# The causal triangle of the first attention's row maxima: from TensorE mask matmuls to fused VectorE instructions

## The chip, the cores and the metric

One core of a Trainium2 chip runs the whole program. The metric is the device time of one execution in microseconds (us); a lower one is better. The core has TensorE (PE, with its weight loads as PEld), VectorE (DVE), ScalarE (ACT), GpSimd (POOL) and a queue of DMA issues on SyncE (SP). Each works through its own instructions in order, and they wait for each other by semaphores.

## The reference

The program is a two-layer block. Only the attention of the first layer is touched:

```
xn = layernorm(x)                         # x: 8 sequences of 256 rows, 256 columns
q, k, v = split(xn @ W_qkv)               # 16 heads of 16
attn = q @ k.T / 4 + alibi_bias + causal_mask   # -inf where j > i
attn = softmax(attn)
s = (attn @ v) @ W_o
x = x + s * silu(ffn0(xn))
# then the second layer: attention of 16 heads of 128, a mixture of experts, x = x + s * silu(...)
```

## The kernel before

The first layer runs as eight batches, one for each sequence, from about 20 to 400 us of the span; `batch(b, ...)` of each engine writes the order out by hand. A batch holds the projections, the attention, the feed-forward (`up`, `down`, with `hidden` on VectorE), the normalisation of the finished sequence b - 1 and its router. The 16 heads form 4 groups of 4; the heads of a group lie on 32 partitions each, so the four matmuls of a group use four quarters of the array.

Softmax needs each query's maximum over its allowed keys. The kernel computes the scores twice. First, `scores(b, g)` on TensorE puts queries on partitions: for each head bank `six[:, h]` takes 256 columns for the late queries (128 to 255, all keys) and 128 columns for the early ones (0 to 127, the first 128 keys). In each of the two the last 128 columns are the diagonal block, where the triangle applies. `maxima(b, g)` on VectorE takes the negated maxima into `nmax`; `maxima_T` on TensorE transposes them (line 433); `queries_max` on VectorE adds them to the queries as a further row (line 1276, `qB`); and `scores_T` on TensorE computes the scores again, with keys on partitions, the maximum already subtracted and its own mask matmuls (line 440), for ScalarE's exponential. The chain within a group is thus TensorE, VectorE, TensorE, VectorE, TensorE, and the orders by hand put other work between the links.

On TensorE, between scores and maxima_T stand: in group 0 two projections of 12 matmuls each; in group 1 the mix of group 0, one `up` of 12 matmuls and two transposes; in group 2 the same kind; in group 3 also the router's six logit matmuls. On VectorE, the maxima stand in group 0 behind the last router step, in group 1 behind `gate_s` (line 1316), in group 2 behind the normalisation of the former sequence (`normalise`, line 1241, which waits for rs of GpSimd), and in group 3 behind the normalisation of the next sequence. In groups 0 and 1 VectorE has little queued ahead of the maxima, in groups 2 and 3 it has a good deal.

The semaphores: `s0_ps` says that a group's scores are there, `max0` that its maxima are, `nmaxT_ps` that they are transposed, and `exp0` that ScalarE has read the transposed scores, before which `scores` must not write the banks again. `three` (lines 390 to 392) is a product in three matmuls, of high and low parts.

Of the kernel before, what the change touches and what calls it, by code (L numbers as in the profile page):

```python
# [25 lines left out]
BF16 = mybir.dt.bfloat16  # L26
ALU = mybir.AluOpType
ACT = mybir.ActivationFunctionType
AX = mybir.AxisListType

P = 128
NB, T, D = 8, 256, 256
TT, KD = T // P, D // P
NT = NB * TT
H0, E0 = 16, 16
GH = 4
NG = H0 // GH
VW = P // GH
# [17 lines left out]
def build(nc, x, pack_qk, pack_vo, pack_w1, pack_w3, pack_w2, pack_attn, pack_experts, pack_shared, gate_b, q_norm, k_norm,  # L56
          rope_cosT, rope_sinT, ident_c, hadamard_c, tri_add_c, tri_mul_c, q_row_c, k_rows_c, before_c, route_c, out):
    ctx = ExitStack()
    with ctx:
        def sem(name):  # L60
            return ctx.enter_context(nc.semaphore(name))
# [5 lines left out]
        six = ctx.enter_context(nc.psum_tensor("six", [P, 6, 512], F32))  # L67
# [16 lines left out]
        def region(start, end):  # L84

            at = [start]

            def put(name, shape, dt=F32):
                size = math.prod(shape[1:]) * (2 if dt == BF16 else 4)
                t = nc.alloc_sbuf_tensor_at(name, shape, dt, offset=at[0])  # L90
                at[0] += (size + 31) // 32 * 32
                assert at[0] <= end, (name, at[0], end)
                return t
            return put
# [4 lines left out]
        sa = region(LOW, LATE)  # L99
# [3 lines left out]
        w2_h, w2_l = sa("w2_h", [P, NJ, D], F32R), sa("w2_l", [P, NJ, D], F32R)  # L103
        w2_a = sa("w2_a", [P, NJ * D])
        hadamard_r = sa("hadamard_r", [P, P], F32R)
        ident_b, tri_add, tri_addT = sa("ident_b", [P, P], BF16), sa("tri_add", [P, 2, P], BF16), sa("tri_addT", [P, 2, P], BF16)
        q_row, k_rows = sa("q_row", [P, 1]), sa("k_rows", [P, NG, T])
        cosT_sb, sinT_sb, norm_w = sa("cosT_sb", [P, H1]), sa("sinT_sb", [P, H1]), sa("norm_w", [P, 2])
        st0, mv0, ve0, rs0 = sa("st0", [P, TT, 6]), sa("mv0", [P, TT, 2]), sa("ve0", [P, TT]), sa("rs0", [P, TT])
# [2 lines left out]
        qA, qB, kA = sa("qA", [P, NG, T]), sa("qB", [P, NG, T]), sa("kA", [P, NG, T])  # L112
        nmax = sa("nmax", [P, TT, P])
# [9 lines left out]
        sa = region(LATE, TOP)  # L123
# [88 lines left out]
        xT0l_sb, xT1l_sb, max0, z0_sb, hid_sb, hidl_sb = (sem(n) for n in (  # L212
            "xT0l_sb", "xT1l_sb", "max0", "z0_sb", "hid_sb", "hidl_sb"))
# [26 lines left out]
        def after(eng, s, value):  # L240

            if isinstance(value, int) and value <= 0:
                return
            eng.wait_ge(s, value)
# [12 lines left out]
        hadamard, tri_add32 = y0[:, 0, 0:P], y0[:, 0, P:2 * P]  # L257
# [129 lines left out]
        def _(pe):  # L387
# [25 lines left out]
            def scores(b, g):  # L413

                pe.wait_ge(qA_sb, 2 * b + g // 2 + 1)
                pe.wait_ge(kA_sb, 2 * b + g // 2 + 1)
                after(pe, exp0, 4 * b + g)
                for h in range(GH):
                    pe.matmul(six[:, h, P:3 * P], ident_b[:], tri_add[:].rearrange("p c k -> p (c k)"),
                              start=True, stop=False, skip_group_check=True)  # L420
                for h in range(GH):
                    r = slice(h * VW, (h + 1) * VW)
                    pe.matmul(six[:, h, 0:T], qA[r, g, P:T], kA[r, g, :], start=False, stop=True, skip_group_check=True)
                for h in range(GH):
                    r = slice(h * VW, (h + 1) * VW)
                    last = pe.matmul(six[:, h, T:T + P], qA[r, g, 0:P], kA[r, g, 0:P], start=False, stop=True,
                                     skip_group_check=True)
                last.then_inc(s0_ps, 1)

# [135 lines left out]
            def batch(b, par, first, final):  # L565
                t = b - 1
                if first:
                    pe.wait_ge(consts_made, 1)
                scores(b, 0)
                pe.wait_ge(kA_sb, 2 * b + 1)  # L570
                queries(b, 1)
# [12 lines left out]
                if not first:  # L584
                    project_out(t, banks[0][:, :])
                scores(b, 1)
                mix(b, 0, par)
                if first:
# [21 lines left out]
                after(pe, gf_sb, b)  # L610
                down(b, 0)
                scores(b, 2)
                mix(b, 1, par)
                pe.wait_ge(hid_sb, 8 * b + 2)
# [57 lines left out]
            t = NB - 1  # L672
# [529 lines left out]
        def _(dve):  # L1202
# [61 lines left out]
            def maxima(b, g):  # L1264

                dve.wait_ge(s0_ps, 4 * b + g + 1)
                after(dve, nmaxT_ps, 4 * b + g)
                dve.tensor_reduce(out=nmax[:, 1, E0 + 1::VW], in_=six[:, 0:GH, 0:T], axis=AX.X, op=ALU.max, negate=True)
                dve.tensor_reduce(out=nmax[:, 0, E0 + 1::VW], in_=six[:, 0:GH, T:T + P], axis=AX.X, op=ALU.max,
                                  negate=True).then_inc(max0, 1)  # L1270

            def queries_max(b, g):

# [124 lines left out]
            def batch(b, first, final):  # L1398
# [6 lines left out]
                def ffn_lo(n, wl, wh):  # L1405
                    dve.wait_ge(wa_hi, n + 1)
                    lo(wl[:].rearrange("p k c -> p (k c)"), raw[:, n % 2, :], wh[:].rearrange("p k c -> p (k c)"))\
                        .then_inc(wa_lo, 1)

                maxima(b, 0)  # L1410
                if not first:
                    gate_out(t)
# [5 lines left out]
                if first:  # L1418
                    ffn_lo(2, w1_l, w1_h)
                    ffn_lo(3, w3_l, w3_h)  # L1420
                maxima(b, 1)
                beside(0)
                queries_max(b, 1)
# [12 lines left out]
                if not first:  # L1436
                    normalise(t, xn1, mv1, rs1, rs1_sb, xn1_sb)
                maxima(b, 2)
                queries_max(b, 2)
                hidden(b, 3)  # L1440
# [27 lines left out]
            norm_T0(0)  # L1468
            dve.wait_ge(consts_loaded, 16 * N_CONST)
            dve.tensor_copy(ident_b[:], ident[:])  # L1470
            dve.tensor_copy(tri_add[:], tri_add32[:].unsqueeze(1).to_broadcast([P, 2, P]))
            dve.tensor_scalar(out=tri_addT[:], in0=tri_mul[:].unsqueeze(1).to_broadcast([P, 2, P]), scalar1=1.0,
                              scalar2=1e30, op0=ALU.subtract, op1=ALU.mult)
            dve.tensor_copy(hadamard_r[:], hadamard[:])
# [16 lines left out]
            t = NB - 1  # L1491
# [446 lines left out]
```

## Time and profile before

| | |
|---|---|
| time, median of 3 runs | 1307.63 us (1307.0 to 1309.41) |
| the profiled execution | 1307.02 us, span 1305.2 us |
| mean granted TensorE clock | 0.985 |
| TensorE busy | 1234.5 us, 95% of the span |
| VectorE busy | 865.4 us, 66% |
| ScalarE busy | 599.8 us, 46% |
| GpSimd busy | 490.9 us, 38% |
| chain that ended last | PE 86%, DVE 8%, ACT 2%, issue 2% |

The page gives the busy time of each engine, with matmul ends modelled; the chain that ended last is followed back from the last instruction, at each step to what released it. A timeline lists instructions in order of start, with the idle time of the engine before them and what ended it in square brackets. A row marked x4 or x8 holds several instructions: its duration runs from the first start to the last end, so that it overlaps the row that follows.

### The profile page before, as it was taken

The numbers are of one execution on the slowest core, as the hardware profiler recorded it, in microseconds if no ns is written. First come the engines' busy times: TensorE is split into PE (matmuls) and PEld (weight loads), VectorE is DVE, ScalarE is ACT, GpSimd is POOL, SyncE is SP. The second block draws the span as 40 slices with busy tenths as digits, with TensorE's granted clock in tenths as the row PEclk, the third lists the DMA queues.
The fourth block names the chain that finished last, engine by engine and source line by source line (L and its number), as shares of the span: only waits on it lengthen the run. The fifth ranks groups of instructions, "written<-read, shape, count | busy, mean of one in ns | idle before, by whom it ended". The sixth has DMA issues, their size and how long they took to land.

```text
span 1305.2 us, 25390 instructions
## 1 busy us (share of the span) xinstructions
PE 1234.5 (95%) x9326; PEld 1083.8 (83%) x9326; DVE 865.4 (66%) x1733; ACT 599.8 (46%) x1351; POOL 490.9 (38%) x488
## 2 busy tenths in 40 slices
PE   5699999999998789999989999999999999999996
PEld 4588888888887667777768999999999999999995
DVE  4647667667666744434457878888887766777685
ACT  3333333333433345555545555454554545555452
POOL 0122432442341400000027766767675444454441
PEclk9799999999999989999999999999999999999998
DMA  6764144234102943333330111102010000000010
GB/s 212 266 230 154 66 154 154 91 128 162 42 34 98 353 159 105 103 105 105 103 114 28 62 30 56 34 25 65 26 58 9 32 2 1 2 1 1 1 33 33
DMA packets 63672, 112.18 MB, mean 86 GB/s; under 512 B 6976, under 2 KB 36032, under 8 KB 62016
## 3 DMA queue, kind: packets, MB, share of 16 engines
q1 hardware_dynamic: 57408, 93.79, 20.5%
q0 software_dynamic: 6144, 16.79, 4.0%
q8 instruction: 77, 1.26, 0.4%
q14 instruction: 43, 0.35, 0.1%
HBM read 49.86 MB, written 60.69 MB: 85 GB/s over the span
## 4 chain that ended last, share of the span: by engine, by line
PE 86%; DVE 8%; ACT 2%; issue 2%; DMA 0%; POOL 0%; SPq 0%; POOLq 0%; DVEq 0%; ACTq 0%
PE bank L703 7%; PE six L720 6%; PE bank L781 4%; PE bank L779 4%; PE bank L780 4%; PE six L817 4%; PE bank L390 4%; PE bank L392 3%; PE bank L391 3%; PE bank L852 2%; PE bank L854 2%; PE bank L853 2%; PE bank L792 2%; PE bank L791 2%; PE bank L793 2%; PE six L818 2%
## 5 line engine op out<-in xcount | busy, mean ns | idle before, releaser
L1604 DVE TENSOR_TENSOR sq<-xs 128x512 f32<-128x512 f32 x128 | 131.1, 1025 | 39.2 <-ACT xs L1147 39.2
L1801 POOL TENSOR_TENSOR rstd<-msq,half_pow 128x8 f32<-128x8 f32 x64 | 105.9, 1655 | 96.2 <-DVE msq L1611 94.3
L1128 ACT ACTIVATE pT<-six,rstd 128x256 f32<-128x256 f32 x128 | 60.7, 475 | 172.1 <-PE six L818 172.1
L1813 POOL TENSOR_TENSOR pT<-pT,tri_mul 128x512 f32<-128x512 f32 x64 | 82.0, 1281 | 147.2 <-ACT pT L1175 147.2
L1738 POOL TENSOR_TENSOR hid_l<-hid,hid_h 128x256 fp32r<-128x256 f32 x64 | 48.0, 750 | 229.4 <-ACT hid_h L950 229.4
L703 PE MATMUL bank<-experts,xT 128*128 x316 | 109.8, 470 | 0.8 <-ACT xT L1072 0.8
L779 PE MATMUL bank<-bw_h,xT1h 128*128 128x512 f32 x256 | 105.6, 412 | 0.7 <-issue 0.7
L781 PE MATMUL bank<-bw_l,xT1h 128*128 128x512 f32 x256 | 100.3, 392 | 0.0
L780 PE MATMUL bank<-bw_h,xT1l 128*128 128x512 f32 x256 | 100.0, 390 | 0.0
L1213 DVE TENSOR_TENSOR yT1l<-six,yT1h 128x512 fp32r<-128x512 f32 x64 | 44.2, 691 | 83.0 <-ACT yT1h L1180 83.0
L1804 POOL TENSOR_TENSOR qn<-xs,rstd 128x256 f32<-128x256 f32 x128 | 91.5, 736 | 5.0
L1606 DVE TENSOR_REDUCE ssq<-sq 128x4 f32<-128x512 f32 x128 | 87.8, 686 | 4.4
L1152 ACT ACTIVATE v<-bank 128x512 f32<-128x512 f32 x64 | 38.3, 598 | 109.1 <-PE bank L793 109.1
L1147 ACT ACTIVATE xs<-bank 128x512 f32<-128x512 f32 x128 | 78.1, 610 | 11.7 <-PE bank L781 4.3
L720 PE MATMUL six<-experts,zT 128*128 x316 | 81.5, 380 | 1.2 <-DVE zT L1553 1.2
L852 PE MATMUL bank<-bw_h,yT1h 128*128 128x256 f32 x256 | 77.9, 304 | 3.8 <-DVE yT1l L1213 3.8
L1833 POOL DMA_INDIRECT yg<-cells_scratch,slots_all x64 | 75.5, 1180 | 14.8 <-issue 14.8
L1839 POOL MEMSET v<- 128x16 f32 x1 | 0.1, 125 | 214.5 <-PE six L720 214.5
L390 PE MATMUL bank<-xT0h,w_h 128*128 128x256 f32 x256 | 76.0, 297 | 2.7 <-DVE w_l L1213 2.5
L817 PE MATMUL six<-qT,kT 128*128 128x256 f32 x256 | 76.4, 380 | 2.1 <-ACT qT L1169 1.2
L1553 DVE COPY zT<-six 128x256 f32<-128x256 f32 x95 | 40.3, 424 | 56.7 <-PE six L711 56.7
L791 PE MATMUL bank<-bw_h,xT1h 128*128 128x256 f32 x256 | 77.3, 302 | 0.0
(282 smaller groups left out, 3934.6 us busy)
## 6 DMA issues: line engine op xcount, KB each, us to landing
cells_scratch<-zeros SPq DMA_DIRECT2D x8, 4352.0 KB, 14.8
xg<-cells_scratch SPq DMA_DIRECT2D x79, 128.0 KB, 2.0
cells_scratch<-y SPq DMA_DIRECT2D x79, 128.0 KB, 1.7
experts<-pack_experts_dram SPq DMA_DIRECT2D x16, 608.0 KB, 11.8
raw<-pack_attn_dram SPq DMA_DIRECT2D x8, 1024.0 KB, 5.3
raw<-pack_w_dram SPq DMA_DIRECT2D x2, 1024.0 KB, 4.9
xT_scratch<-xT1h_c SPq DMA_DIRECT2D x8, 256.0 KB, 2.1
xT_scratch<-xT1l_c SPq DMA_DIRECT2D x8, 256.0 KB, 2.9
```

The costliest lines, as they stand in the source:

```text
L390: pe.matmul(o, wh, mh, start=first, stop=False)
L703: last = pe.matmul(banks[j % 2][:, 0:2 * HE], xT[:, j % 2, k, :], weights(e, k * 2 * HE, 2 * HE), start=k == 0, stop=k == KD - 1)
L720: last = pe.matmul(six[:, 4 + r, 0:D], zT[:, r, c, :], w, start=c == 0, stop=c == 1)
L779: pe.matmul(banks[tt][:, :], xT1h[:, k, c], w[0][:, k, :], start=k == 0, stop=False)
L780: pe.matmul(banks[tt][:, :], xT1l[:, k, c], w[0][:, k, :], start=False, stop=False)
L781: last = pe.matmul(banks[tt][:, :], xT1h[:, k, c], w[1][:, k, :], start=False, stop=k == KD - 1)
L791: pe.matmul(o[:, tt, :], xT1h[:, k, c], w[0][:, k, :], start=k == 0, stop=False)
L817: pe.matmul(s_b[:, 0, h * T:(h + 1) * T], kT1[:, r, h, 0:P], qT1[:, r, h, :], start=True, stop=True)
L852: pe.matmul(o[:, tt, :], yT1h[:, r, h, c], w[0][:, h, :], start=h == 0, stop=False)
L1604: dve.tensor_tensor(out=sq[:, tt, :], in0=x_qk, in1=x_qk, op=ALU.mult).then_inc(sq_sb, 1)
L1801: pool.tensor_tensor(out=rstd[:, r, :], in0=msq[:, r, :], in1=half_pow[:], op=ALU.pow).then_inc(rstd_sb, 1)
L1804: last = pool.tensor_tensor(out=qn[:, r, tt, :, :], in0=xs[:, r, tt, 0, :, :], in1=rstd[:, r, 4 * tt:4 * tt + 2].unsqueeze(2).to_broadcast ...
```

## The change

`scores` no longer begins with four mask matmuls (identity times triangle, bf16, 256 columns, one per head); the score matmuls start their banks themselves. `maxima` no longer takes two reductions over the four heads together, of 1024 and 512 elements per partition. It issues, for each head and each half, one fused instruction: it adds the mask (now float, 256 wide, its first half zero), multiplies by -1, writes the result back over the scores in PSUM, and keeps the minimum, which is the negated maximum, in an accumulator that goes to one column of `nmax`. `scores_T` keeps its own mask matmuls.

```diff
@@ buffers
-        ident_b, tri_add, tri_addT = sa("ident_b", [P, P], BF16), sa("tri_add", [P, 2, P], BF16), sa("tri_addT", [P, 2, P], BF16)
+        ident_b, tri_add, tri_addT = sa("ident_b", [P, P], BF16), sa("tri_add", [P, T]), sa("tri_addT", [P, 2, P], BF16)
@@ TensorE, scores
                 for h in range(GH):
-                    pe.matmul(six[:, h, P:3 * P], ident_b[:], tri_add[:].rearrange("p c k -> p (c k)"),
-                              start=True, stop=False, skip_group_check=True)
+                    r = slice(h * VW, (h + 1) * VW)
+                    pe.matmul(six[:, h, 0:T], qA[r, g, P:T], kA[r, g, :], start=True, stop=True, skip_group_check=True)
                 for h in range(GH):
                     r = slice(h * VW, (h + 1) * VW)
-                    pe.matmul(six[:, h, 0:T], qA[r, g, P:T], kA[r, g, :], start=False, stop=True, skip_group_check=True)
-                for h in range(GH):
-                    r = slice(h * VW, (h + 1) * VW)
-                    last = pe.matmul(six[:, h, T:T + P], qA[r, g, 0:P], kA[r, g, 0:P], start=False, stop=True,
+                    last = pe.matmul(six[:, h, T:T + P], qA[r, g, 0:P], kA[r, g, 0:P], start=True, stop=True,
                                      skip_group_check=True)
                 last.then_inc(s0_ps, 1)
@@ VectorE, maxima
-                dve.tensor_reduce(out=nmax[:, 1, E0 + 1::VW], in_=six[:, 0:GH, 0:T], axis=AX.X, op=ALU.max, negate=True)
-                dve.tensor_reduce(out=nmax[:, 0, E0 + 1::VW], in_=six[:, 0:GH, T:T + P], axis=AX.X, op=ALU.max,
-                                  negate=True).then_inc(max0, 1)
+                for h in range(GH):
+                    e = h * VW + E0 + 1
+                    for t, s, mask in ((1, six[:, h, 0:T], tri_add[:]), (0, six[:, h, T:T + P], tri_add[:, P:T])):
+                        last = dve.tensor_tensor_reduce(out=s, in0=s, in1=mask, scale=-1.0, scalar=1e30, op0=ALU.add,
+                                                        op1=ALU.min, accum_out=nmax[:, t, e:e + 1])
+                last.then_inc(max0, 1)
@@ VectorE, constants
-            dve.tensor_copy(tri_add[:], tri_add32[:].unsqueeze(1).to_broadcast([P, 2, P]))
+            dve.memset(tri_add[:, 0:P], 0.0)
+            dve.tensor_copy(tri_add[:, P:T], tri_add32[:])
```

TensorE, from the last `down` matmul ahead of group 2's scores to the mix of group 1 (`pT`, `v`), before:

```order
L478 MATMUL six<-w_l,hid_h 128x256
L419 MATMUL six<-tri_add,ident_b 128x256 [waits exp0,kA_sb,qA_sb]
L419 MATMUL six<-tri_add,ident_b 128x256 x3
L423 MATMUL six<-kA,qA 128x256 x4
L426 MATMUL six<-kA,qA 128x128 x4
L458 MATMUL six<-pT_80,v_78 32x256 [waits y0_sb,exp0]
```

The same place in the changed kernel, where code behind the edit has a line number smaller by three:

```order
L475 MATMUL six<-w_l,hid_h 128x256
L420 MATMUL six<-kA,qA 128x256 [waits exp0,kA_sb,qA_sb]
L420 MATMUL six<-kA,qA 128x256 x3
L423 MATMUL six<-kA,qA 128x128 x4
L455 MATMUL six<-pT_80,v_78 32x256 [waits y0_sb,exp0]
```

The four mask matmuls are gone, their waits stand at the first score matmul, and nothing else has moved.

VectorE, from the normalisation ahead of group 2's maxima to the addition to the queries, before:

```order
L1241 TENSOR_SCALAR xn_97<-x_all,mv_93,rs_95 128x256 [waits rs1_sb]
L1241 TENSOR_SCALAR xn_97<-x_all,mv_93,rs_95 128x256
L1268 TENSOR_REDUCE nmax<-six 128x4 [waits nmaxT_ps,s0_ps]
L1269 TENSOR_REDUCE nmax<-six 128x4
L1276 TENSOR_TENSOR qB<-six,qA 128x256 [waits sT0_ps,nmaxT_ps]
```

And now, the first head of four (the rows from `six,nmax` to the second `nmax` stand four times in all, the later three without a wait); a row that only writes `nmax 128x1` is the read of the accumulator, an instruction of its own:

```order
L1238 TENSOR_SCALAR xn_97<-x_all,mv_93,rs_95 128x256 [waits rs1_sb]
L1238 TENSOR_SCALAR xn_97<-x_all,mv_93,rs_95 128x256
L1268 ISA six,nmax<-six,tri_add 128x256 [waits nmaxT_ps,s0_ps]
L1268 ISA nmax 128x1
L1268 ISA six,nmax<-six,tri_add 128x128
L1268 ISA nmax 128x1
```

Two instructions have become sixteen at the same place in the queue, between the same neighbours.

## Rows read from the trace of the kernel before

**Rows 1.** Page, busy us (share of the span) and instructions of each engine:

```profile
PE 1234.5 (95%) x9326; PEld 1083.8 (83%) x9326; DVE 865.4 (66%) x1733; ACT 599.8 (46%) x1351; POOL 490.9 (38%) x488
```

**Rows 2.** Windows view: stretch, length, busy us by engine, clock, DMA share:

```profile
core 0: us, PE busy (x) PEld busy (x) DVE busy (x) ACT busy (x) POOL busy (x), PEclk, DMA share, GB/s
60.00:400.00 340.00, 330.81 (x3437) 288.53 (x3436) 222.63 (x556) 127.23 (x265) 109.81 (x134) 1.00 0.34 124
```

**Rows 3.** Waits of TensorE, 92 to 400 us: total, times, longest:

```profile
PE bank L400 <- DVE hid L1287: 4.5, 6, 0.8
PE bank L390 <- DVE xT0l L1213: 3.1, 6, 0.5
```

**Rows 4.** Timeline of TensorE, 140 to 183 us: start, duration, instruction:

```profile
140.46 0.28 PE L533 MATMUL bank<-wvo_l,yT0h 128*128 128x256 f32 x1
140.58 0.61 PE L419 MATMUL six<-tri_add,ident_b 128*128 128x256 bf16 x4
141.12 0.71 PE L423 MATMUL six<-kA,qA 32*128 32x256 f32 x8
141.66 0.40 PE L426 MATMUL six<-kA,qA 32*128 32x128 f32 x8
...
144.53 0.38 PE L433 MATMUL six<-ident,nmax 128*128 128x128 f32 x2
...
150.92 0.40 PE L426 MATMUL six<-kA,qA 32*128 32x128 f32 x8
...
153.79 0.38 PE L433 MATMUL six<-ident,nmax 128*128 128x128 f32 x2
...
167.34 0.28 PE L392 MATMUL bank<-xT0l,w_h 128*128 128x256 f32 x1
167.56 0.64 PE L458 MATMUL six<-pT,v 128*32 128x256 f32 x8
...
182.85 0.38 PE L433 MATMUL six<-ident,nmax 128*128 128x128 f32 x2
```

**Rows 5.** Timeline of VectorE, 142 to 182 us, idle before in brackets:

```profile
142.12 1.23 DVE L1268 TENSOR_REDUCE nmax<-six 128x4 f32<-128x1024 f32 x1 [0.59 <-PE six L426]
143.26 0.68 DVE L1269 TENSOR_REDUCE nmax<-six 128x4 f32<-128x512 f32 x1
144.95 0.43 DVE L1276 TENSOR_TENSOR qB<-six,qA 128x256 f32<-128x256 f32 x1 [1.01 <-PE six L433]
...
145.74 0.42 DVE L1287 TENSOR_TENSOR hid<-bank,th 128x256 f32<-128x256 f32 x1
146.08 0.20 DVE L1293 RECIPROCAL rden<-six 128x8 f32<-128x8 f32 x1
...
147.60 0.14 DVE L1223 COPY waited<-ident 128x1 f32<-128x1 f32 x1
147.66 0.74 DVE L1225 BATCH_NORM_STATS2 st<-x_all 128x6 f32<-128x256 f32 x2
148.44 0.15 DVE L1228 COPY waited<-st 128x1 f32<-128x1 f32 x1
148.51 0.24 DVE L1230 BATCH_NORM_AGGREGATE mv<-st 128x2 f32<-128x6 f32 x2
...
151.07 0.73 DVE L1241 TENSOR_SCALAR xn<-x_all,mv,rs 128x256 f32<-128x256 f32 x2 [0.34 <-POOL rs L1723]
151.72 1.22 DVE L1268 TENSOR_REDUCE nmax<-six 128x4 f32<-128x1024 f32 x1
152.86 0.68 DVE L1269 TENSOR_REDUCE nmax<-six 128x4 f32<-128x512 f32 x1
...
155.57 0.29 DVE L1296 TENSOR_TENSOR y<-six,rden 128x128 f32<-128x128 f32 x1
155.78 0.74 DVE L1225 BATCH_NORM_STATS2 st<-x_all 128x6 f32<-128x256 f32 x2
...
181.15 0.68 DVE L1269 TENSOR_REDUCE nmax<-six 128x4 f32<-128x512 f32 x1
```

## The prediction

> **What bounds the kernel now.** I read the page's busy shares first: TensorE is busy for 1234.5 us, 95% of the span of 1305.2 us [rows 1]. The changed code runs only in the first attention, whose 32 groups (8 batches, 4 groups of 4 heads) lie between 20 and 400 us. From 60 to 400 us, TensorE is busy 330.8 of 340 us at a granted clock of 1.00 (2.4 GHz) and VectorE 222.6 us, 65% [rows 2]. So the question is not whether VectorE has room on average, for it has, but whether it has room between the two points where TensorE needs its answer. The waits of TensorE from 92 to 400 us say where it stands today: 4.5 us for hid and 3.1 us for xT0l, both at the end of a batch, and nothing for the maxima [rows 3]. Third, I read the two engines' timelines through one batch, the third (b = 2), from 132 to 180 us, and into group 0 of the next, and measured for each group how long after VectorE's last maximum TensorE comes to transpose it. That slack decides the case.
>
> **What is removed on TensorE.** Per group, four mask matmuls. In row order the last projection starts at 140.46, the first mask matmul at 140.58 and the first score matmul at 141.12, so the four hold the queue for 0.54 us [rows 4]. Something of that returns: a 4-byte matmul of 32 rows or columns behind the three-pass projections starts 0.22 us after the last of them (167.34 to 167.56) where the mask matmul started after 0.12 us, so 0.10 us comes back [rows 4]. The gain, G, is 0.54 - 0.10 = 0.44 us per group, 14 us over 32 groups, if all of it were on the path.
>
> **What is added on VectorE.** Two instructions per group become sixteen: four fused ones of 256 elements, four of 128 and, behind each, a one-column read of the accumulator; the order of the changed kernel shows them. No row of the trace shows the fused instruction or that read, so both are bounded by neighbours.
>
> The old pair takes from 142.12 to 143.26 + 0.68 = 143.94, that is 1.82 us [rows 5]. For the new chain the spacing of starts counts, since neighbours without a wait overlap: a 256-element two-input instruction lasts 0.42 us, but the next starts 0.34 us after it (145.74, 146.08); one of 128 elements lasts 0.29 us and the next starts after 0.21 us (155.57, 155.78); a one-column instruction lasts 0.14 to 0.15 us and the next starts after 0.06 to 0.07 us (147.60, 147.66; 148.44, 148.51) [rows 5]. I take 0.34, 0.21 and 0.07: 4 x (0.34 + 0.21) + 7 x 0.07, and 0.14 for the last read in full, is 2.83 us. The maxima then come E = 2.83 - 1.82 = 1.01 us later after their start.
>
> The bounds of E: if every fused instruction and every read must end before the next starts, 4 x (0.42 + 0.29) + 8 x 0.14 = 3.96 us and E = 2.14. If the reads cost nothing, 4 x 0.55 + 0.08 = 2.28 us and E = 0.46. As the far end below, if only elements cost anything: the two reductions start 1.14 us apart for 1024 elements, 1.1 ns each, so 1536 elements take 1.7 us and E = -0.1. I stay near the spacing rows, since they are of the same engine, the same sizes and likewise without waits.
>
> The Trainium skill (Vector Engine (DVE) Microarchitecture Reference, Measured stream behaviour on trn2) gives 1.0417 ns per column and about 75 ns per instruction after overlap. As an estimate that makes 1536 x 1.0417 ns + 16 x 75 ns = 2.80 us of starts, about 2.88 us to the end of the last read, E = 1.06; the time would then be 1319.5 us instead of the forecast below. No row here shows the read itself.
>
> **What of it lies on the path.** The maxima end; TensorE transposes them (L433); VectorE adds them to the queries (L1276); TensorE computes the transposed scores. Allowing 0.05 us from one engine to the other (the transposes end at 144.53 + 0.38, the addition starts at 144.95), the slack ahead of L433 is [rows 4, 5]:
> - group 0: maxima end 181.15 + 0.68 = 181.83, L433 at 182.85: 0.97 us
> - group 1: 143.94, L433 at 144.53: 0.54 us
> - group 2: 152.86 + 0.68 = 153.54, L433 at 153.79: 0.20 us
> - group 3 stands as group 2 does: 0.20 us
>
> Here is the choice that matters: which groups keep G. In groups 0 and 1, VectorE idles until the scores arrive (0.59 us before group 1's maxima, released by L426 [rows 5]), so the maxima start earlier when the mask goes. Group 0 keeps 0.40 us of G, group 1 all 0.44 us. In group 2 the scores are there at 150.92 + 0.40 = 151.32, but the maxima start at 151.72, behind the normalisation (L1241), which waited for GpSimd's rs and before that for the last group's transposes [rows 4, 5]. That chain does not move with the mask. TensorE comes 0.44 us earlier to a transpose whose input is later by E: the gain turns into waiting. Group 3's maxima stand behind the other normalisation in the same way.
>
> A batch therefore moves by -0.40 - 0.44 + (E - 0.97) + (E - 0.54) + 2 x (E - 0.20), a bracket below zero counting as zero in the first two. With E = 1.01: -0.84 + 0.04 + 0.47 + 1.62 = +1.29 us. Nothing absorbs it behind: the end of the batch is a chain ScalarE, VectorE (router), TensorE, which starts from group 3's scores, and its two waits [rows 3] move along whole. Eight batches taken alike are +10.3 us. The first batch differs (the weights' butterfly is on VectorE, its maxima of group 1 are fully on the path) and the last has no second normalisation; I set these off against each other.
>
> **Edits at nothing.** The float mask is made by a memset and a copy in place of one cast, in the start-up. The matmuls' start flags change no duration. The scores written back to PSUM have no reader, since the transposed scores overwrite them after max0. The DMAs are as they were, and code after 400 us is the same; it moves as a whole.
>
> The profiled execution took 1307.02 us (span 1305.2 us and 1.8 us around it), 0.6 us under the median of 1307.63 us. On the median the forecast is 1307.6 + 10.3 = 1317.9, **1318 us**.
>
> **The rivals.** By the same line for a batch, times eight:
> - **The reads are exposed.** Each main instruction drains before its read, E = 2.14: -0.84 + 1.17 + 1.60 + 3.88 = 5.81 us per batch, 46 us, 1354 us. For it: the accumulator is complete only with the last element. Against it: all rows of neighbours without a wait overlap by 0.08 us [rows 5]. The Trainium skill (VectorE: DVE Perf Modes, The DRAIN you can't avoid) says that the next operation does not start until the pipe is empty; by that rule this rival holds, and the trace speaks against it, with starts 0.34 us apart where one lasts 0.42 us. Chance 0.15, spread from 1337 to 1354 us.
> - **Writing scores back in place in PSUM halves the rate.** Then 1536 x 1.1 ns = 1.7 us more, E = 2.7 and about 8 us per batch, some 1371 us. No VectorE row writes PSUM, so nothing speaks for it. Chance 0.03.
> - **Cheap reads: nothing much changes.** E = 0.46 gives -0.84 + 0.52 = -0.32 us per batch, 1305 us; E = 0.7 gives +0.32 us, 1310 us. It needs reads under about 0.03 us; no one-column row is that short. Chance 0.13.
> - **Faster: TensorE's gain survives.** The point is E = 0.59, where 3E = 0.84 + 0.54 + 0.40: if the new chain takes under 2.41 us from first start to last end, TensorE's 0.44 us in groups 0 and 1 outweigh the waits in groups 2 and 3. With E = -0.1 the maxima are never late in groups 0 and 1, and groups 2 and 3 give 0.3 us each: -1.44 us per batch, 1296 us. For it: 95% busy TensorE [rows 1] and 14 us less work there. Against it: 1536 elements and eight fixed costs already make 2.28 us before any read. Chance 0.07.
>
> **How the numbers follow.** The forecast (E from 0.7 to 1.6, 1310 to 1337 us) has 0.62. About 0.2%, 2.6 us, is what a measurement of this kernel can tell from no change: that is 1305.0 to 1310.2 us. Faster has 0.08 (the last rival and the edge of the one before), the same 0.12, slower 0.80. The range of 1306 to 1345 us leaves out some 0.08 below and 0.12 above.
>
> **What the changed profile would show.** TensorE busy falls by the mask matmuls, about 14 us by its queue; new waits of TensorE at the transposes of the maxima, none in group 0, about 0.5 us in group 1 and E - 0.20 + 0.44 = 1.25 us in groups 2 and 3, 3 us per batch and 24 us in all; VectorE's group from first start to last end 2.8 us; each batch after the first 1.3 us longer; nothing changed after the attention. Wrong would be: starts of the fused instructions spaced by more than 0.36 us or the reads by more than 0.09 us (then dearer), or a VectorE start in groups 2 and 3 that follows the scores and not the normalisation (then G is kept there too).

## The result and the profile after

The changed kernel takes 1313.55 us (median of 5 runs, 1313.16 to 1315.22), the one before 1307.63 us: 5.9 us or 0.46% slower, ratio 1.0046 with a 95% interval of 1.0031 to 1.0061. The forecast was slower by 10.3 us. The span of the profiled execution went from 1305.2 to 1312.1 us.

The page after, busy time of each engine as in [rows 1], and the chain that ended last by engine:

```profile
PE 1229.0 (94%) x9198; PEld 1078.9 (82%) x9198; DVE 891.4 (68%) x2182; ACT 600.0 (46%) x1351; POOL 489.7 (37%) x488
PE 76%; DVE 15%; ACT 4%; issue 3%; POOL 1%; DMA 0%; SPq 0%; ACTq 0%; DVEq 0%; POOLq 0%
```

128 matmuls are gone, VectorE has 449 rows more, and the chain has moved: TensorE carried 86% of it before, now 76%, and VectorE 15% in place of 8%. The maxima themselves (L1268) are 4% of it.

The forms of the new work, line, engine, operation, count, busy us and mean ns of one:

```profile
L1268 DVE CUSTOM_DVE_ANT_0 six<-six,tri_add 128x256 f32<-128x256 f32 x128 | 58.5, 457 | 5.4 <-PE six L423 4.5
L1268 DVE CUSTOM_DVE_ANT_0 six<-six,tri_add 128x128 f32<-128x128 f32 x128 | 42.5, 332 | 0.0
L1268 DVE DVE_READ_ACCUMULATOR2_ANT nmax<- 128x1 f32 x256 | 36.4, 142 | 0.0
```

What counts is the distance of starts. VectorE's timeline in group 1 of the third batch, which answers to the first rows of [rows 5]:

```profile
143.14 0.43 DVE L1268 CUSTOM_DVE_ANT_0 six<-six,tri_add 128x256 f32<-128x256 f32 x1
143.49 0.14 DVE L1268 DVE_READ_ACCUMULATOR2_ANT nmax<- 128x1 f32 x1
143.49 0.33 DVE L1268 CUSTOM_DVE_ANT_0 six<-six,tri_add 128x128 f32<-128x128 f32 x1
143.74 0.14 DVE L1268 DVE_READ_ACCUMULATOR2_ANT nmax<- 128x1 f32 x1
143.74 0.47 DVE L1268 CUSTOM_DVE_ANT_0 six<-six,tri_add 128x256 f32<-128x256 f32 x1
144.12 0.14 DVE L1268 DVE_READ_ACCUMULATOR2_ANT nmax<- 128x1 f32 x1
144.12 0.33 DVE L1268 CUSTOM_DVE_ANT_0 six<-six,tri_add 128x128 f32<-128x128 f32 x1
...
145.63 0.14 DVE L1268 DVE_READ_ACCUMULATOR2_ANT nmax<- 128x1 f32 x1
```

A read starts together with the next fused instruction; a pair of 256 elements and its read takes 0.38 us from start to start (the first 0.35), one of 128 takes 0.25. The group lasts from 143.14 to 145.77, 2.63 us, where it was 1.82: E, the time by which the maxima of a group take longer, is 0.81 us, not 1.01. The other groups show the same to 0.01 us, but for one in the third batch (2.72 us).

The waits of TensorE from 92 to 400 us, as in [rows 3]:

```profile
PE six L430 <- DVE nmax L1268: 11.8, 13, 0.9
PE bank L400 <- DVE hid L1287: 4.6, 6, 0.8
PE bank L390 <- DVE xT0l L1210: 3.2, 6, 0.5
```

The two old waits at the end of a batch are as they were; a new one has come for the maxima, listed for 13 groups, those with number 2 and 3. TensorE's timeline in groups 1 and 2 of the third batch (L430 is the former L433):

```profile
142.66 0.40 PE L423 MATMUL six<-kA,qA 32*128 32x128 f32 x8
...
145.83 0.44 PE L430 MATMUL six<-ident,nmax 128*128 128x128 f32 x2
...
151.82 0.40 PE L423 MATMUL six<-kA,qA 32*128 32x128 f32 x8
...
154.47 0.38 PE L463 MATMUL six<-ident,yt 128*128 128x128 f32 x2
155.76 0.44 PE L430 MATMUL six<-ident,nmax 128*128 128x128 f32 x2 [0.91 <-DVE nmax L1268]
```

In group 2 the view gives TensorE 0.91 us of idle time, counted from the modelled end of the matmul before. The distance of starts says more. In the kernel before, the transposes of the maxima start 0.21 us behind those of `yt`:

```profile
153.58 0.38 PE L466 MATMUL six<-ident,yt 128*128 128x128 f32 x2
153.79 0.38 PE L433 MATMUL six<-ident,nmax 128*128 128x128 f32 x2
```

Now they start 1.29 us behind them, so the wait is 1.08 us. In group 1 (`yt` at 145.32, maxima at 145.83) it is 0.30 us, though that row shows no idle time. VectorE's own row says why the maxima are late there:

```profile
152.42 0.74 DVE L1238 TENSOR_SCALAR xn<-x_all,mv,rs 128x256 f32<-128x256 f32 x2 [0.33 <-POOL rs L1724]
153.07 0.43 DVE L1268 CUSTOM_DVE_ANT_0 six<-six,tri_add 128x256 f32<-128x256 f32 x1
```

The scores were there at 151.82 + 0.40 = 152.22; the maxima start at 153.07, behind the normalisation, which waited for GpSimd.

For the rest I use one measure. There are 32 transposes of the maxima; the start of each, less the start of the same one in the kernel before, is how far the program has moved by then, and the difference from one to the next is what a group gave. Mean of batches 1 to 6, us:

| kernel | group 0 | group 1 | group 2 | group 3 | batch | first batch, at its group 3 |
|---|---|---|---|---|---|---|
| changed | -0.47 | -0.16 | +0.66 | +0.68 | +0.71 | +1.20 |
| forecast for it | -0.40 | +0.03 | +0.81 | +0.81 | +1.29 | taken as the others |
| the same line with E = 0.81 | -0.40 | -0.17 | +0.61 | +0.61 | +0.65 | |

At the last transpose of the eighth batch the program is 5.5 us behind (400.37 us before, 405.88 after), and the last of the second layer's query and key projections starts 5.9 us later (1271.5 before, 1277.4 after): nothing behind the attention gives or takes much.

The first batch has a loss of its own. Its group 1 moves by +1.4 us, and not because of the maxima. There, TensorE waits ahead of `up` for the low part of the weights (`w_l`), which comes when it comes. Without the mask matmuls TensorE arrives earlier and waits longer. The first `up` matmul and the transposes of the maxima, before and after:

```profile
32.16 0.39 PE L390 MATMUL bank<-xT0h,w_h 128*128 128x256 f32 x1 [2.46 <-DVE w_l L1213]
33.91 0.42 PE L433 MATMUL six<-ident,nmax 128*128 128x128 f32 x2
```

```profile
31.67 0.58 PE L390 MATMUL bank<-xT0h,w_h 128*128 128x256 f32 x1 [2.97 <-DVE w_l L1210]
34.82 0.63 PE L430 MATMUL six<-ident,nmax 128*128 128x128 f32 x2
```

And the windows view of 33 to 36 us, before and after (the granted clock is the third number from the end):

```profile
33.00:36.00 3.00, 3.00 (x28) 2.82 (x26) 3.00 (x5) 0.58 (x2) 0.00 (x0) 1.00 0.00 0
33.00:36.00 3.00, 3.00 (x16) 3.00 (x16) 2.75 (x11) 0.39 (x1) 0.00 (x0) 0.50 0.00 0
```

Behind the wait of 2.46 us the clock stayed at 1.00 (2.4 GHz), behind that of 2.97 us it was 0.50 (1.2 GHz), and the same matmuls take 3.15 us up to the transposes in place of 1.75. The last maximum was there at 34.16 us, 0.66 us before its transpose.

### The profile page after: what moved, and what is told of

Same layout as the page of the kernel before. It is cut to its first block, busy times and chain, and to the rows that moved or that the text cites. A ratio compares the mean times of both kernels' runs of the same rounds, so it can differ in the third digit from the quotient of the medians.

```text
span 1312.1 us, 25583 instructions
## 1 busy us (share of the span) xinstructions
PE 1229.0 (94%) x9198; PEld 1078.9 (82%) x9198; DVE 891.4 (68%) x2182; ACT 600.0 (46%) x1351; POOL 489.7 (37%) x488
## 4 chain that ended last, share of the span: by engine, by line
PE 76%; DVE 15%; ACT 4%; issue 3%; POOL 1%; DMA 0%; SPq 0%; ACTq 0%; DVEq 0%; POOLq 0%
PE bank L700 7%; PE six L717 6%; PE bank L778 4%; PE bank L776 4%; PE bank L777 4%; PE six L814 4%; DVE six L1268 4%; PE bank L851 2%; PE bank L849 2%; PE bank L850 2%; PE bank L789 2%; PE bank L788 2%; PE bank L790 2%; PE six L828 2%; PE six L829 2%
## 5 line engine op out<-in xcount | busy, mean ns | idle before, releaser
L1605 DVE TENSOR_TENSOR sq<-xs 128x512 f32<-128x512 f32 x128 | 131.1, 1024 | 39.3 <-ACT xs L1144 39.3
L1268 DVE CUSTOM_DVE_ANT_0 six<-six,tri_add 128x256 f32<-128x256 f32 (+1 forms) x256 | 82.3, 394 | 5.4 <-PE six L423 4.5
```

Source lines behind the costliest of these rows:

```text
L1268: last = dve.tensor_tensor_reduce(out=s, in0=s, in1=mask, scale=-1.0, scalar=1e30, op0=ALU.add, op1=ALU.min, accum_out=nmax[:, t, e:e + 1])
L1605: dve.tensor_tensor(out=sq[:, tt, :], in0=x_qk, in1=x_qk, op=ALU.mult).then_inc(sq_sb, 1)
```

## The experiments

My theory: the change moves a batch by TensorE's 0.44 us where the maxima start with the scores, and by VectorE's E beyond the slack, and the loss is made in groups 2 and 3. Its rivals: TensorE's saved time counts wholly, VectorE's total load counts wherever it lies, or the position of the maxima does not matter.

**TensorE's half alone.** `scores` as in the changed kernel, `maxima` as before, so that the mask is left out of the maxima and the result is another one (part of the edit):

```diff
-                    pe.matmul(six[:, h, P:3 * P], ident_b[:], tri_add[:].rearrange("p c k -> p (c k)"),
-                              start=True, stop=False, skip_group_check=True)
...
-                    last = act.activation(pT0[:, g % 2, h:h + 2, :], six[:, h:h + 2, 0:3 * P], ACT.Exp)
+                    last = act.activation(pT0[:, g % 2, h:h + 2, :], six[:, h:h + 2, 0:3 * P], ACT.Exp, scale=0.01)
```

> Only TensorE's half of the change: the four mask matmuls per group are gone, VectorE keeps its two plain reductions. It leaves the mask out of the maxima, and the exponential gets a scale of 0.01 so that the sums stay finite; neither changes an instruction's size. My theory (the maxima of groups 2 and 3 stand behind a normalisation that does not follow the mask, so only groups 0 and 1 keep their 0.4 us): -0.40 - 0.44 us per batch, about -7 us, 1300.5 us, with new waits of TensorE for the maxima of groups 2 and 3 of about 0.25 us each. Rival (TensorE is the bound and all 14 us of its removed work come back): 1293.5 us and no new waits.

Measured: 1298.43 us against 1308.07 us for the kernel before on the same chip, ratio 0.9921 (0.9907 to 0.9934), -9.6 us. By groups -0.49, -0.45, -0.21, -0.14, a batch -1.28 us. Neither time expected was met, and the fault was in how I applied my own line: with E = 0 the last bracket is below zero, 2 x (0 - 0.20), and I had written nothing for it. With it a batch is -0.84 - 0.40 = -1.24 us, close to what came. So groups 2 and 3 keep, of the 0.44 us, only the slack of 0.20; the rest is lost to a start that does not move:

```profile
148.46 0.74 DVE L1238 TENSOR_SCALAR xn<-x_all,mv,rs 128x256 f32<-128x256 f32 x2 [0.33 <-POOL rs L1720]
149.11 1.22 DVE L1265 TENSOR_REDUCE nmax<-six 128x4 f32<-128x1024 f32 x1
```

Here the scores end at 147.85 + 0.40 = 148.25 us, and the plain reductions start at 149.11. The waits of about 0.25 us that were expected in groups 2 and 3 are there, though the waits view has none: the transposes of the maxima start 0.47 us behind those of `yt` (150.51 and 150.98) and not 0.21, so TensorE waits 0.26 us. The first batch has the lower clock too (0.50 from 33 to 36 us), with VectorE's work as it was: its group 1 moves by +1.4 us here as well.

**VectorE's half alone.** The mask matmuls stay, `maxima` is the fused one with a float mask of its own:

```diff
+            dve.memset(tri_f[:, 0:P], 0.0)
+            dve.tensor_copy(tri_f[:, P:T], tri_add32[:])
...
-                dve.tensor_reduce(out=nmax[:, 1, E0 + 1::VW], in_=six[:, 0:GH, 0:T], axis=AX.X, op=ALU.max, negate=True)
...
+                        last = dve.tensor_tensor_reduce(out=s, in0=s, in1=mask, scale=-1.0, scalar=1e30, op0=ALU.add,
+                                                        op1=ALU.min, accum_out=nmax[:, t, e:e + 1])
```

> Only VectorE's half: the mask matmuls stay, and the fused instructions add the mask once more. With the extra time E = 0.81 us read from the changed kernel (2.63 us for a group against 1.82), my theory gives 0 + 0.27 + 0.61 + 0.61 us per batch, about +12 us, 1319.5 us. Rival (VectorE has idle time enough, the loss of the change comes from something else, such as the start of the banks or PSUM traffic): at most +2 us.

Measured: 1320.73 us, ratio 1.0098 (1.0083 to 1.0114), +12.7 us. By groups +0.05, +0.28, +0.66, +0.67: E = 0.81 against the slacks of 0.97, 0.54 and 0.20 us. From the second batch on, E against slack accounts for the cost within 0.06 us a group, and the way that `scores` starts its banks needs no part in it. That the output goes to PSUM does have a part, inside E, as shown further down. In the first batch, where the mask matmuls are kept, TensorE waits 2.46 us for `w_l`, the clock stays at 1.00, and group 1 moves by +0.81 us, which is E in full.

The two halves add up to +3.1 us and not to the +5.9 us of the change. In groups 2 and 3 each half alone makes use of the slack of 0.20 us, and together they can use it once: by TensorE's half it is worth 0.35 us per batch (0.21 + 0.14), 2.8 us over eight.

**The two normalisations behind the maxima**, in the changed kernel:

```diff
-                if not first:
-                    normalise(t, xn1, mv1, rs1, rs1_sb, xn1_sb)
                 maxima(b, 2)
                 queries_max(b, 2)
+                if not first:
+                    normalise(t, xn1, mv1, rs1, rs1_sb, xn1_sb)
...
-                if not final:
-                    normalise(b + 1, xn0, mv0, rs0, rs0_sb, xn0_sb)
                 maxima(b, 3)
                 queries_max(b, 3)
                 hidden(b, 5)
                 heads_out(b, 2)
+                if not final:
+                    normalise(b + 1, xn0, mv0, rs0, rs0_sb, xn0_sb)
```

> The changed kernel with VectorE's two normalisations moved from ahead of the maxima of groups 2 and 3 to behind them (that of the former sequence behind queries_max of group 2, that of the next sequence behind heads_out of group 2). My theory: groups 2 and 3 then start their maxima when the scores arrive, as group 1 does, and give -0.17 us each in place of +0.67; a batch is then -0.47 - 3 x 0.17 = -1.0 us, about -7 us on the kernel before, 1300.5 us. Rival (the position does not matter, VectorE's longer work is what counts): within 2 us of the changed kernel's 1313.5 us.

Measured: 1301.67 us, ratio 0.9957 (0.9943 to 0.9970), 6.4 us faster than the kernel before, where the changed one was 5.9 us slower: 12 us between the two. By groups -0.48, -0.15, -0.12, +0.02, a batch -0.73 us where -1.0 was expected. VectorE now idles until the scores are there:

```profile
150.25 0.43 DVE L1268 CUSTOM_DVE_ANT_0 six<-six,tri_add 128x256 f32<-128x256 f32 x1 [0.19 <-PE six L423]
```

The wait for the maxima that the view shows in [rows 3]'s stretch is small:

```profile
PE six L430 <- DVE nmax L1268: 1.8, 7, 0.3
```

By the distance of starts TensorE still waits 0.3 us in groups 1 and 2 and 0.4 us in group 3.

Group 3 gives +0.02 and not -0.17: its maxima now stand behind `hidden(b, 4)`, which starts after the low part of the former sequence's transposes, and start at 159.19 us with the scores complete at 158.28.

**The control**: the same move in the kernel before.

> Control: the same move of the two normalisations in the kernel before, mask matmuls and plain reductions kept. TensorE does not wait for the maxima there today, so my theory gives no change, 1307.6 us within 1.5 us. Rival (the order of before is slow by itself and the gain of the moved version is the move's alone): 6 us or more faster, about 1301 us.

Measured: 1307.75 us against 1308.07, ratio 0.9997 (0.9988 to 1.0006), every group of batches 1 to 6 within 0.06 us of zero, and the means within 0.01. The move alone is worth nothing; it is the condition under which the change pays.

The remaining eight runs fell on two other chips, where the kernel before itself takes 1337.1 us and not 1308 (no trace of it there). Their traces share a stall that the first chip's don't have, shown further down. It sits in group 1 from the third batch on, so the groups around it can still be read, and the totals only with care.

**What makes a step of the chain 0.38 us.** Four forms, one for each group:

```diff
+                o = six if g % 2 == 0 or b == 0 else w2_a[:, 0:GH * 3 * P].rearrange("p (h c) -> p h c", h=GH)
...
+                        if g < 2:
+                            last = dve.tensor_tensor_reduce(out=o[:, h, c], in0=s, in1=mask, scale=-1.0, scalar=1e30, op0=ALU.add,
+                                                            op1=ALU.min, accum_out=nmax[:, t, e:e + 1])
+                        else:
+                            last = dve.scalar_tensor_tensor(out=o[:, h, c], in0=s, scalar=1.0, in1=mask, op0=ALU.mult, op1=ALU.add)
```

> One look at what makes a step of the fused chain 0.38 us (256 elements) and 0.25 us (128) long, where plain neighbours took 0.34 and 0.21 us. In the changed kernel, from the second batch on, each group takes another form: group 0 fused with its accumulator read and written to PSUM, as it is; group 1 the same but written to SBUF; group 2 a plain two-operation instruction without an accumulator, written to PSUM; group 3 the same written to SBUF. The maxima of groups 2 and 3 are left out, the exponential is scaled by 0.01. If the read costs the 0.04 us, groups 0 and 1 step by 0.38 and 0.25 us and groups 2 and 3 by 0.34 and 0.21 us. If the write into PSUM costs it, groups 0 and 2 are the slow ones. The time of the whole is of no interest.

VectorE's timeline: fused to PSUM, fused to SBUF, then the plain form to PSUM and to SBUF, eight instructions merged into a row (from the first start to the last end):

```profile
133.88 0.47 DVE L1270 CUSTOM_DVE_ANT_0 six<-six,tri_add 128x256 f32<-128x256 f32 x1
134.27 0.14 DVE L1270 DVE_READ_ACCUMULATOR2_ANT nmax<- 128x1 f32 x1
134.27 0.33 DVE L1270 CUSTOM_DVE_ANT_0 six<-six,tri_add 128x128 f32<-128x128 f32 x1
134.51 0.14 DVE L1270 DVE_READ_ACCUMULATOR2_ANT nmax<- 128x1 f32 x1
...
146.77 0.42 DVE L1270 CUSTOM_DVE_ANT_0 w_a<-six,tri_add 128x256 f32<-128x256 f32 x1
147.12 0.08 DVE L1270 DVE_READ_ACCUMULATOR2_ANT nmax<- 128x1 f32 x1
147.12 0.28 DVE L1270 CUSTOM_DVE_ANT_0 w_a<-six,tri_add 128x128 f32<-128x128 f32 x1
147.33 0.08 DVE L1270 DVE_READ_ACCUMULATOR2_ANT nmax<- 128x1 f32 x1
...
148.99 0.08 DVE L1270 DVE_READ_ACCUMULATOR2_ANT nmax<- 128x1 f32 x1
156.95 2.21 DVE L1273 SCALAR_TENSOR_TENSOR six<-six,tri_add 128x256 f32<-128x256 f32 x8
166.11 2.20 DVE L1273 SCALAR_TENSOR_TENSOR w_a<-six,tri_add 128x256 f32<-128x256 f32 x8
```

Neither expectation holds alone. The plain instruction writes into PSUM at no extra cost (2.21 us against 2.20), and a fused one with its read costs hardly more than a plain one when it writes to SBUF (steps of 0.35 and 0.21 us, the whole group 146.77 to 149.07, 2.30 us). Only both together make 0.38 and 0.25 us and a read of 0.14 us. A fused instruction to PSUM without a read was not run, so it isn't shown whether the read itself or the fused instruction is what the write to PSUM slows. That outputs alternate between the two memories, or that the read waits for the write into PSUM, would look alike here.

**The fused instructions with an SBUF scratch**, from the second batch on:

```diff
+                o = six if b == 0 else w2_a[:, 0:GH * 3 * P].rearrange("p (h c) -> p h c", h=GH)
...
-                        last = dve.tensor_tensor_reduce(out=s, in0=s, in1=mask, scale=-1.0, scalar=1e30, op0=ALU.add,
+                        last = dve.tensor_tensor_reduce(out=o[:, h, c], in0=s, in1=mask, scale=-1.0, scalar=1e30, op0=ALU.add,
```

> The changed kernel with one edit: from the second batch on the fused instructions write to the SBUF scratch. The line of the prediction with E = 0.48: -0.47 - 0.44 + 2 x (0.48 - 0.20) = -0.35 us per batch, seven times, and the first batch as in the changed kernel (+1.2 us): about -1 us on the kernel before, 1307 us. Rival (the place of the output changes single rows but not the group, since the reads then cost their own time): like the changed kernel, +5.5 us.

Measured: 1345.69 us against 1337.15, ratio 1.0065 (1.0046 to 1.0085), 8.5 us slower where 1 us faster was expected. By groups it does what the line says: -0.49 in group 0, -0.46 in group 1 of the second batch (the one without the stall), +0.29 in group 2 and +0.35 in group 3 in the median.

**Both mends together:**

> Both mends together: the fused instructions write their result to a scratch in SBUF (from the second batch on) and the two normalisations stand behind the maxima. With steps of 0.34 and 0.21 us the extra time is E = 2.30 - 1.82 = 0.48 us, under group 1's slack of 0.54 us, so that every group keeps its 0.44 us: -1.8 us per batch for seven batches, about -12 us on the kernel before (1296 us where that takes 1308). Rival (E is not what holds the gain back any more): like the version with the moved normalisations alone, -6.4 us.

Measured: 1334.89 us against 1337.15, ratio 0.9986 (0.9975 to 0.9996), -2.3 us where -12 were expected. By groups -0.48, -0.46 (second batch), -0.46, -0.33: every group but the last keeps its whole 0.44 us, as expected. The total is again about 10 us above the line.

**TensorE's half with the moved normalisations**, twice:

> TensorE's half alone (mask left out of the maxima, exponential scaled by 0.01, plain reductions) together with the moved normalisations. With E = 0 and all four groups starting at their scores, each keeps the whole 0.44 us: -0.47 - 3 x 0.44 = -1.8 us per batch, -14 us, about 1294 us, against about -9.6 us measured without the move. Rival (something else in groups 2 and 3 holds the gain back): it stays at 1298.4 us within 1.5 us.

> TensorE's half alone with the moved normalisations, once more for the same reason (mask left out of the maxima, exponential scaled by 0.01): the whole gain that TensorE can give, 4 x 0.44 us per batch, -14 us on the kernel before. Rival: -9.6 us, as without the move.

Measured: 1331.20 against 1337.13 us (ratio 0.9958, 0.9945 to 0.9972), and 1331.37 against 1337.15 (0.9955, 0.9938 to 0.9972), -5.9 and -5.8 us. By groups -0.53, -0.43 and -0.46 (second batch), -0.46, -0.46 (the last two in the median; group 2 of the second of these runs -0.42): with the maxima behind the scores, each group keeps all of it. The total is some 8 us above the line.

**The change in groups 0 and 1 alone**, twice:

```diff
+                if g < 2:
...
+                else:
+                    for h in range(GH):
+                        pe.matmul(six[:, h, P:3 * P], ident_b[:], tri_add[:].rearrange("p c k -> p (c k)"),
+                                  start=True, stop=False, skip_group_check=True)
```

> The change in groups 0 and 1 alone; groups 2 and 3 keep the mask matmuls and the two plain reductions. If the loss sits wholly in groups 2 and 3, a batch gives -0.47 - 0.17 us, the values that the changed kernel shows for these groups, and 0 for the others: -5.1 us on the kernel before, about 1302.9 us. Rival (VectorE's load counts in total, wherever it lies): half of the changed kernel's loss, +3 us, 1311 us.

> The change in groups 0 and 1 alone, once more, because on the chip of the first run even the kernel before took 1337 us. If that chip's stalls of TensorE in group 1 were what covered the effect: -0.47 - 0.17 us per batch, -5 us on the kernel before. If the stalls come with the kernel's own code, it is slower than the kernel before here too.

Measured: 1343.42 against 1337.13 us (ratio 1.0043, 1.0030 to 1.0057), and 1343.19 against 1337.15 (1.0048, 1.0029 to 1.0067): 6 us slower, not 5 faster. Group 0 gives -0.52 us and group 1 of the second batch -0.18, as in the changed kernel. The total decides nothing between theory and rival, because of the stall.

**Group 1's transposes behind half of `up(b, 1)`**, with the moved normalisations (`up` takes the halves to issue as an argument):

```diff
-                maxima_T(b, 1)
                 after(pe, sgf_sb, b)
-                up(b, 1)
+                up(b, 1, (0,))
+                maxima_T(b, 1)
+                up(b, 1, (1,))
```

> The changed kernel with the moved normalisations, and on TensorE group 1's transposes of the maxima moved behind the first six matmuls of up(b, 1), 0.72 us later. Theory: group 1's slack then exceeds E - 0.54, it keeps all of its 0.44 us where it now shows -0.17 us, and the addition of the maxima still ends ahead of the transposed scores, which had about 0.8 us to spare: 8 x 0.27 = 2.2 us faster than the version without the split (1301.7 us), about 1299.5 us. Rival (the later transposes make VectorE and the rest of the batch late): 1301.7 us or slower.

Measured: 1341.37 against 1337.13 us, ratio 1.0031 (1.0018 to 1.0043). In the second batch groups 1 and 2 together give +0.28 - 0.90 = -0.62 us (the transposes of group 1 start 0.72 us later by the edit itself) against -0.16 - 0.12 = -0.28 without the split, so the step works there; its worth as a whole is open.

**The stall on the other two chips.** TensorE's timeline of the last named TensorE-only kernel in group 1 of the third batch, "issue" being time in which nothing that the profile shows was waited for:

```profile
141.00 0.43 PE L457 MATMUL six<-pT,v 128*32 128x128 f32 x5 [0.79 <-issue]
142.43 0.41 PE L457 MATMUL six<-pT,v 128*32 128x128 f32 x3 [1.00 <-issue]
```

And the windows view of the version with both mends, around the same place:

```profile
141.00:144.00 3.00, 1.85 (x16) 0.50 (x16) 0.24 (x1) 0.38 (x1) 0.97 (x1) 1.00 0.25 87
144.00:147.00 3.00, 3.00 (x16) 3.00 (x15) 2.67 (x17) 0.46 (x2) 1.29 (x1) 0.52 0.00 0
147.00:150.00 3.00, 3.00 (x28) 2.72 (x30) 2.00 (x6) 0.99 (x3) 0.08 (x1) 0.92 0.02 5
```

In the first of these windows TensorE has 16 matmuls, where the kernel before has 44 in the same stretch on the first chip. In the next the granted clock is 0.52, near its lower level of 1.2 GHz. The TensorE-only kernel shown above kept its clock at 1.00 at this place, and its group 1 moved by +3.3 us against the kernel before on the first chip. In the later batches every trace from these chips has the clock at 0.50 for about 3 or 7 us around the stall, and group 1 moves by +4.4 to +7.2 us. Behind the attention these traces are another 4 to 6.5 us longer.

Five kernels without mask matmuls in group 1 came out 8 to 13 us above the line there. The first batch on the first chip suggests why: there the kernels with mask matmuls wait 2.46 us and keep the clock, and those without wait 2.97 us and lose it. If the kernel before keeps its clock in the stalls, it loses less in each of the six. That isn't shown, for there is no trace of it from such a chip, and the changed kernel itself was not run there. What can be said is that on each of these two chips the change in groups 0 and 1 alone was 6 us slower, and that the line, made from one chip's trace, does not give the totals there. The cause of the stall is open.

## Why the prediction was right, and where it was off

- **The direction and the mechanism held.** VectorE's half costs 12.7 us by itself, TensorE's gives 9.6 us by itself, and together they make the change 5.9 us slower. The loss is made in groups 2 and 3 (+1.34 us per batch), and groups 0 and 1 gain (-0.63 us). The slacks of 0.97, 0.54 and 0.20 us, read from one batch, were met by VectorE's half alone within 0.06 us.
- **E was mis-sized: 1.01 us forecast, 0.81 measured.** The step at fault took the accumulator's read as a neighbour that spaces starts by 0.07 us like a one-column copy. Fused instruction and read together take 0.04 us more than the 0.34 and 0.21 us, and only where the output goes to PSUM. The steps of 0.34 and 0.21 us for the main instructions were right, as the SBUF form shows (0.35 and 0.21). E enters three times per batch, so 0.20 us less makes 0.60 us, with the 0.04 us that E = 1.01 gave group 0 0.64 us less per batch, and 5.1 us in all; this is the 4.4 us between forecast and result, and a bit more. With E = 0.81 the line gives 8 x 0.65 = 5.2 us.
- **G = 0.44 us** was right: groups that keep it show -0.44 to -0.52 us.
- **"Groups 2 and 3 keep nothing of G"** was right for this change, and the move of the normalisations bears out the reason: 12 us between two kernels that differ only in where these stand, and nothing between the same two orders in the kernel before.
- **Taking eight batches alike** came out by luck. The first gave +1.2 us and the last +0.05, since its group 3 has no normalisation ahead; against +0.71 for the others these offset each other, as was assumed, but not for the reason given. "Its maxima of group 1 are fully on the path" holds for VectorE's half alone (+0.81 us). In the changed kernel group 1 of the first batch moves by +1.4 us because TensorE's clock fell to its lower level behind a longer wait for `w_l`, and the maxima were ready 0.66 us early. The prediction has no term for a clock that depends on the work taken away.
- **The signs to look for.** The wait in groups 2 and 3 was forecast at 1.25 us, and by E = 0.81 at 1.05; the idle time in the rows is 0.91, but the distance of starts gives 1.08, and 0.30 in group 1 against 0.27 by the line. The waits view books 13 us in all, the distances some 18 us (groups 1 to 3), where 24 were forecast with the larger E. So the waits view undercounts: it starts at the modelled end of the matmul before, and a wait of up to 0.3 us is not listed at all. TensorE's busy time fell by 5.5 us (1234.5 to 1229.0), not by 14. That sign was badly chosen; even TensorE's half alone shows only 8.8 us less (1225.7), and with the lower clock of the first batch the same matmuls are busy for longer.
- **The rivals.** Exposed reads (E = 2.14) fell: starts overlap, here 0.35 us apart at a duration of 0.43. The Trainium skill (VectorE: DVE Perf Modes, The DRAIN you can't avoid) says that the next operation does not start until the pipe is empty, and goes on that one that is not held starts earlier; these rows agree with the second, and the prediction's use of the first alone, as the rule by which this rival holds, was too strong. The halved rate in PSUM fell too: eight plain instructions take 2.21 us to PSUM. Cheap reads came near: a read took some 0.04 us and not 0.07, where this rival wanted under 0.03, and E = 0.81 lies just above its 0.7. "Faster below E = 0.59" was not reached by the change, but it is the right bound: the SBUF scratch has E = 0.48, and by groups a batch gets 0.3 us shorter (-0.49 - 0.46 + 0.29 + 0.35), though its total on another chip was 8.5 us longer. The Trainium skill's 75 ns per instruction (Vector Engine (DVE) Microarchitecture Reference, Measured stream behaviour on trn2) gave E = 1.06; the measured 0.81 disagrees, as far as the read counts as an instruction there. Counted for the main instructions alone, the same figures give, as an estimate, 0.34 and 0.21 us from start to start, and the SBUF form agrees with 0.35 and 0.21.

The best version measured on the first chip that computes the right result is the changed kernel with the moved normalisations, 1301.67 us, faster than both kernels compared. The one with the SBUF scratch too is better by its groups, but its total was taken on another chip only, 2.3 us faster than the kernel before there.

## What to carry to other kernels

Moving work from a busy engine to an idle one pays only as far as the idle engine's answer has slack before it is needed; read that slack at each place where the answer is used, not from the busy shares. Ask also what the answer's start follows: where it follows something else in the queue, time saved upstream turns into waiting, and a reorder that is worth nothing by itself can be what makes the change pay. A fused instruction with an accumulator in SBUF was cheaper when its unwanted output went to SBUF too. And look for waits that grow when work ahead of them is removed: here one of 2.97 us in place of 2.46 came with the lower clock and cost the first batch 1.4 us. Last, check a total on more than one chip before you trust a line drawn from one trace.

## What the runs showed of the hardware

- A fused instruction of VectorE with its accumulator read costs hardly more than a plain one when its output goes to SBUF: eight pairs take 2.30 us, eight plain ones 2.20, with a read of 0.08 us and starts 0.35 and 0.21 us apart for 256 and 128 elements. When the output goes to PSUM the starts are 0.38 and 0.25 us apart, the read lasts 0.14 us, and eight pairs take 2.63 us.
- VectorE's plain instruction reads and writes the same PSUM columns in place as fast as it writes to SBUF: 2.21 and 2.20 us for eight.
- Behind a wait of TensorE of 2.46 us the granted clock stayed at 1.00, behind one of 2.97 us at the same place it was 0.50. All three kernels with mask matmuls in group 1 of which there is a trace show the first, in the first batch, and all eleven without them the second.
- Chips differ: 1308 us on one, 1337 us on two others for the same kernel. On these, variants of it show TensorE with 1.8 to 3.7 us of idle time in group 1 of each batch from the third on, mostly without a cause that the profile shows, and in most of these batches the lower clock level for about 3 or 7 us.
